# Graph kernel on one core: edge rows made of aligned fours, four gather slots a row, built in the first stage

## The reference

```python
xl, xr, e = x @ Wl.T + bl, x @ Wr.T + br, edge_attr @ We.T
m = xl[src] + xr[dst] + e
score = jnp.where(m > 0, m, 0.2 * m) @ att
es = jnp.exp(score - segment_max(score, dst)[dst])
alpha = es / (segment_sum(es, dst)[dst] + 1e-16)
out = segment_sum(alpha[:, None] * xl[src], dst)
```

## Time and profile before

| | |
|---|---|
| median of 3 runs | 15386.39 us (15376.81 to 15424.71) |
| profiled execution, span | 15438.3 us |
| TensorE, VectorE busy | 7512.3, 6521.2 us (49%, 42%) |
| ScalarE, GpSimd busy | 3580.5, 7851.1 us (23%, 51%) |
| DMA | mean 72 GB/s, 1912984 packets |
| mean granted TensorE clock | 0.605 of full speed |

### The profile page before, as it was taken

How to read it: one execution, slowest core, us unless ns; L and a number is a source line. 1 busy time by engine, 2 the same in 40 slices (tenths; PEclk the granted TensorE clock), 3 DMA queues, 4 the chain that set the end, 5 groups by cost and what they waited for, 6 DMA issues and landing times. The chain is left out here.

```text
span 15438.3 us, 178521 instructions
## 1 busy us (share of the span) xinstructions
PE 7512.3 (49%) x38527; PEld 6783.9 (44%) x38528; DVE 6521.2 (42%) x11789; ACT 3580.5 (23%) x4864; POOL 7851.1 (51%) x8083
## 2 busy tenths in 40 slices
PE   0555555545555555355455554444444434545442
PEld 0544544544455544344444433444444334444442
DVE  3344444444444544333333343444444634434343
ACT  0222222212222222122222212222222122222220
POOL 3455555525555554356556615555455155555551
PEclk9566666656666666555555555555555555665565
DMA  2333333333333333222222233333333243333331
GB/s 69 76 78 80 78 75 76 78 62 80 76 78 78 80 78 62 41 46 47 47 45 49 47 101 82 76 75 78 74 76 76 73 117 83 85 83 85 83 74 22
DMA packets 1912984, 1106.77 MB, mean 72 GB/s; under 512 B 1548686, under 2 KB 1593762, under 8 KB 1911874
## 3 DMA queue, kind: packets, MB, share of 16 engines
q1 hardware_dynamic: 1654786, 718.42, 19.1%
q0 software_dynamic: 257568, 382.66, 12.6%
HBM read 1003.35 MB, written 96.52 MB: 71 GB/s over the span
## 5 line engine op out<-in xcount | busy, mean ns | idle before, releaser
L1006 POOL DMA_INDIRECT ds_gat<-table_d,ds_idx x1568 | 1508.6, 962 | 1562.1 <-issue 803.9
L1006 POOL DMA_INDIRECT as_gat<-table_a,as_idx x1568 | 1529.5, 975 | 1254.5 <-DMA as_idx<-in_srcT 721.1
L1006 POOL DMA_INDIRECT bs_gat<-table_b,bs_idx x1568 | 1538.6, 981 | 1199.0 <-DMA bs_idx<-idx_d 680.0
L1006 POOL DMA_INDIRECT es_gat<-table_e,es_idx x1568 | 1523.7, 972 | 1195.7 <-issue 578.3
L1006 POOL DMA_INDIRECT cs_gat<-table_c,cs_idx x1568 | 1532.7, 978 | 1088.9 <-issue 544.8
L1271 PE MATMUL cs_psA<-cs_ahot,cs_wtd 128*68 128x128 f32 x3136 | 670.8, 400 | 434.0 <-ACT cs_psA L1031 315.3
L1271 PE MATMUL es_psA<-es_ahot,es_wtd 128*68 128x128 f32 x3136 | 619.2, 377 | 406.5 <-ACT es_psA L1031 256.1
L1271 PE MATMUL bs_psA<-bs_ahot,bs_wtd 128*65 128x128 f32 x3136 | 624.2, 361 | 393.8 <-issue 351.3
L1271 PEld LDWEIGHTS cs_psA<-cs_ahot,cs_wtd 128*68 128x68 f32 x3136 | 605.2, 221 | 456.0 <-issue 455.6
L1256 PE MATMUL es_psM<-es_dst,es_hot 128*128 128x64 f32 x3136 | 595.2, 361 | 415.1 <-issue 202.3
L1256 PEld LDWEIGHTS es_psM<-es_dst,es_hot 128*128 128x128 f32 x3136 | 568.7, 275 | 462.2 <-issue 369.8
(11 more groups left out here) (734 smaller groups left out, 16292.6 us busy)
## 6 DMA issues: line engine op xcount, KB each, us to landing
ds_dst<-dst_d SPq DMA_DIRECT2D x1568, 34.0 KB
as_rank<-rel_d SPq DMA_DIRECT2D x196, 256.0 KB
as_dst<-dst_a SPq DMA_DIRECT2D x1568, 32.0 KB
as_ea<-in_eaT SPq DMA_DIRECT2D x196, 256.0 KB
bs_rank<-rel_d SPq DMA_DIRECT2D x196, 256.0 KB
bs_dst<-dst_b SPq DMA_DIRECT2D x1568, 32.0 KB
bs_ea<-in_eaT SPq DMA_DIRECT2D x196, 256.0 KB
cs_rank<-rel_d SPq DMA_DIRECT2D x196, 256.0 KB
```

What stands on the lines that cost most here:

```text
L1006: g_.indirect_dma_start(gat[s][:, j, :], None, table, bass.IndirectOffsetOnAxis(ap=idxS[s][:, j:j + 1].bitcast(U32), axis=0)).then_inc(got ...
```

## The change

Edges are taken four at a time (50000 aligned fours). One row, that is one partition of a tile, is a pair of a four and a destination that occurs in it: it has four gather slots, of which those whose edge has another destination are masked by a penalty (`pen`, -1e37). A four with edges of two destinations makes two rows, so there are at most 50000 + 6249 rows, in T = 440 tiles. A group is 2 tiles, which is again 8 gathers (220 groups), a chunk 8 tiles or four groups (55 chunks). What changes with it:

- `expand` and `collect` work on 2 tiles a group, with one destination window a tile. In a and b the features of the four edges of a row are turned by 4 products (`edges`), copied to SBUF by ScalarE (`eS`), and spread by a second one-hot matrix (`hot`, index 1), since two rows can share a four.
- The maximum over the four slots is taken before the scans (`most`), which so run on a quarter of the partitions. In a, b, c and e the maximum is transposed back (`B`), subtracted from the scores (`lower`) and only then goes through the exponential; in d the scores of all four slots are transposed.
- `weigh` is followed by a sum over the four slots (`wsum`), `flush` handles one tile of 256 columns instead of two of 512.
- `feed` loads the index four groups earlier (`LEAD`); `lag` is 7, in d still 8.
- `prepare` builds the rows on the chip: it counts destinations per four, makes prefix sums, finds by two small gathered searches which fours each tile begins with (`quad`, `lead`), and then, in 55 steps of 8 tiles, loads a window of 128 fours a tile and picks the rows out of it with products (`unpack`, `spans`, `prefix`, `fields`). Indices, types, ranks and masks come from that instead of from the inputs.

The diff, cut to its core:

```diff
+S = 4
+QN = E // S
+GS = 8
+GROUP = GS // S
+CT = 4 * GROUP
+T = -(-(QN + N - 1) // (P * CT)) * CT
...
+                for g in range(VGS):
+                    wait(sp, read, g - 3)
+                    at = load_windows(nc, m["quad"], g * VG, VG, mybir.EngineType.SP, QN - 1)
+                    for j in range(VG):
+                        sp.dma_start(winI[g % 4][:, j, :], t["quads"][bass.ds(at[j], P), :]).then_inc(wind[g % 4], 16)
...
+                def unpack(g):
+                    v.wait_ge(wind[g % 4], (g // 4 + 1) * 16 * VG)
+                    wait(v, vfd, g - 1)
+                    link(v.tensor_copy(winF[g % 2][:, :, 0:3 * S], winI[g % 4][:, :, :]))
...
+                def spans(g):
+                    v.wait_ge(pred, g + 1)
...
+                    v.tensor_tensor(ge[:, :, :], iota, over(lo[:, :], 2, [P, VG, P]), ALU.is_ge)
+                    link(v.tensor_tensor(hot[g % 2][:, :, :], iota, over(hi[:, :], 2, [P, VG, P]), ALU.is_lt))
+                    v.tensor_tensor(hot[g % 2][:, :, :], hot[g % 2][:, :, :], ge[:, :, :], ALU.mult).then_inc(hotted, 1)
...
+                    for j in range(VG):
+                        last = pe.matmul(psV[g % 2][:, j * NF:(j + 1) * NF], hot[g % 2][:, j, :], winF[g % 2][:, j, :], start=True, stop=True)
...
-                    wait(sp, got[s], it * GOT)
-                    sp.dma_start(idxS[s][:, :], idx[:, bass.ds(g * GROUP, GROUP)]).then_inc(idxd[s], 16)
+                    if within(g + LEAD, GROUPS):
+                        feed_idx(*later(it, s, LEAD))
...
+                        quads = load_windows(nc, m["quad"], g * GROUP, GROUP, mybir.EngineType.SP, QN - 1)
+                        for j in range(GROUP):
+                            sp.dma_start(ea[s % 4][:, :, j, :], t["eaT"][:, :, bass.ds(quads[j], P)]).then_inc(eaed[s % 4], 16)
...
-                        for h in range(2):
-                            a.wait_ge(flushed, (k - 2) * 2 + (h + 1))
-                            a.activation(psA[h][0:CW, :], zero[0:CW, :], ACT.Copy).then_inc(zeroed, 1)
+                        a.wait_ge(flushed, k - 1)
+                        a.activation(psA[ks % 2][0:CW, 0:SPAN], zero[0:CW, :], ACT.Copy).then_inc(zeroed, 1)
...
+                def most(c, cs):
+                    v.wait_ge(scored, c * CG + CG)
+                    order = "p s h t -> p h t s" if i == 3 else "p t s h -> p h t s"
+                    v.tensor_reduce(smx[:, :, :], sc[cs][:, :, :, :].rearrange(order), AX_X, ALU.max).then_inc(maxed, 1)
...
+                def lower(xc, xs):
+                    v.wait_ge(backed, xc + 1)
+                    wait(v, alphad, xc)
+                    top = psX[:, BACK:BACK + R].rearrange("p (h t) -> p t h", h=H)
+                    v.tensor_tensor(Dl[:, :, :, :], sc[xs][:, :, :, :], over(top, 2, [P, CT, S, H]), ALU.subtract).then_inc(lowered, 1)
...
+                    v.tensor_reduce(wsum[ks % 2][:, :, :], wtd[:, :, :].rearrange("p (j s) c -> p j c s", s=S), AX_X, ALU.add).then_inc(pooled, 1)
...
+                    for j in range(GROUP):
+                        for x in range(S // 2):
+                            at = (j * (S // 2) + x) * 2 * D
+                            last = pe.matmul(psE[s % 2][:, at:at + 2 * D], ea[s % 4][:, x, j, :], we[:, :], start=True, stop=True)
...
+                            pe.matmul(into, hot[s % 2][:, j, 1, :], eS[s % 2][:, j * S * D:(j + 1) * S * D], start=True, stop=False)
+                            last = pe.matmul(into.rearrange("p (s c) -> p s c", s=S), hot[s % 2][:, j, 0, :],
+                                             over(dsts[s % 4][:, j, :], 1, [P, S, D]), start=False, stop=True)
...
+                    for j in range(GROUP):
+                        last = pe.matmul(at[j], wsum[ks % 2][:, j, :], ahot[ks % 2][:, j, :], start=False, stop=False, skip_group_check=True)
+                    last.then_inc(summed, 1)
```

More of the change, by code:

```diff
@@ L30 @@
 REL = 8
-GROUP = 8
 K = -(-N // P)
@@ new lines, in prepare @@
+        VF = sb("VF", [P, T, NF])
+        kth = sb("kth", [P, T])
+        dl = sb("dl", [P, T, S])
+        val = sb("val", [P, T, S])
+        node = sb("node", [P, T])
+        idxI = sb("idxI", [P, T * S], I32)
+        typI = sb("typI", [P, T * S], I32)
+        nodeT = sb("nodeT", [P, TB, P])
+        new = sb("new", [P, TB, P])
+        cum = sb("cum", [P, TB, P])
+        mask = sb("mask", [P, TB, P], BF16)
+        both = sb("both", [P, TB, 2, P], BF16)
+        tot = sb("tot", [P, 4, TB])
@@ L445, in _ @@
                 pe.wait_ge(made, MADE)
-                pe.wait_ge(sums, 1)
-                pe.matmul(psS[0:ROWS, 0:1], upper[0:ROWS, 0:ROWS], small[0:ROWS, 0:1], start=True, stop=True).then_inc(offs, 1)
-                for b in range(BLK):
-                    pe.wait_ge(back, max(1, b))
-                    pe.transpose(psT[b % 2][:, 0:ROWS], relS[:, b * P:(b + 1) * P], m["ident"][0:ROWS, 0:ROWS]).then_inc(turned, 1)
-                pe.wait_ge(ends, 1)
-                pe.matmul(psS[:, 8:9], pickF[:, :], cumE[:, 0:1], start=True, stop=False)
@@ L454, in _ @@
[L454 to L459 removed]
+                pe.wait_ge(counted, 1)
@@ new lines, in _, with prefix @@
+                pe.matmul(psS[0:EROWS, 0:1], upper[0:EROWS, 0:EROWS], small[0:EROWS, 0:1], start=True, stop=True).then_inc(offs, 1)
+                pe.wait_ge(headed, 1)
+                pe.matmul(psS[:, 8:8 + EROWS], allone[0:EROWS, :], diag[:, :], start=True, stop=True).then_inc(spreadH, 1)
+                def prefix(g):
+                    pe.wait_ge(nqd, g + 1)
+                    wait(pe, hotted, g - 1)
+                    pe.matmul(psP[g % 2][:, 0:VG], upper[:, :], nq[g % 2][:, :], start=True, stop=True).then_inc(pred, 1)
@@ new lines, in fields @@
+                def fields(g):
+                    pe.wait_ge(hotted, g + 1)
+                    wait(pe, taken, g - 1)
+                    for j in range(VG):
+                        last = pe.matmul(psV[g % 2][:, j * NF:(j + 1) * NF], hot[g % 2][:, j, :], winF[g % 2][:, j, :], start=True, stop=True)
+                    last.then_inc(vfd, 1)
+                prefix(0)
+                for g in range(VGS):
+                    if g + 1 < VGS:
+                        prefix(g + 1)
+                    fields(g)
@@ new lines, in _ @@
+                pe.wait_ge(noded, 1)
+                for b, n in blocks():
+                    wait(pe, pulled, b - 1)
+                    pe.transpose(psT[b % 2][0:n, 0:P], node[:, b * P:b * P + n], m["ident"][:, :]).then_inc(turned, 1)
+                    pe.transpose(psT[b % 2][0:n, P:2 * P], VF[:, b * P:b * P + n, 3 * S + 2], m["ident"][:, :]).then_inc(turned, 1)
+                pe.wait_ge(pulled, TB)
+                pe.matmul(psS[:, 128:128 + TB], after[:, :], nodeT[:, :, P - 1], start=True, stop=True).then_inc(shifted, 1)
@@ new lines, in _ @@
+                pe.wait_ge(summed, 1)
+                pe.matmul(psS[:, 144:144 + TB], upper[:, :], tot[:, 0, :], start=True, stop=True)
+                pe.matmul(psS[:, 144 + TB:144 + 2 * TB], allone[:, :], tot[:, 0, :], start=True, stop=True).then_inc(offset, 1)
+                pe.wait_ge(ranked, 2)
+                for b, n in blocks():
+                    wait(pe, back, b - 1)
+                    pe.transpose(psT[b % 2][:, 0:n], new[0:n, b, :], m["ident"][0:n, 0:n]).then_inc(backed, 1)
@@ L462, in masks @@
+                pe.matmul(psS[:, 122:124], allone[:, :], small[:, 2:4], start=True, stop=True).then_inc(placedR, 1)
 def masks(nc, t, d):
@@ L1234, in step @@
                         score(it, s)
+                        if r == CG - 1:
+                            most(it * 3 + c, c)
+                    if i != 3 and r == 2 and live:
+                        lower(xc, xs)
                 rounds(v, step, END)
@@ L1313, in step @@
                         pe.wait_ge(normed, xc + 1)
-                        pe.matmul(psX[:, 256:256 + CT], Al[:, :], m["quart"][:, :], start=True, stop=True).then_inc(backed, 1)
+                        for x in range(S):
+                            last = pe.matmul(psX[:, BACK + x * CT:BACK + (x + 1) * CT], Al[:, x, :], m["quart"][0:R, :], start=True, stop=True)
+                        last.then_inc(backed, 1)
                     if within(k - 1, GROUPS):
```

848 lines of the change are left out of this document (519 added, 329 removed).

## The result

The changed kernel takes 16037.49 us (median of 4 runs, 16021.16 to 16073.24) where the kernel before took 15397.68 us on the same chip: ratio 1.0412, 95% interval 1.0382 to 1.0442. A second measurement on another chip gave 1.0344 (1.0306 to 1.0381). The forecast was 14760 us, the range ended at 15650.

A forecast was written before the change was run, and what follows sets the result against it. Waits bound it, no engine being full: Sync and TensorE crawl while GpSimd issues indirect DMAs without pause. 15438.3 - 969 (streams) + 342 (first stage and masks) = 14811 us, with the profiled execution 52 us above the median: 14760 us, range 13550 to 15650.

The forecast's parts named there:

- What bounds the kernel: Whole kernel: waits, not a full engine; Sync and TensorE slow while GpSimd gathers without pause; VectorE's own work does not slow.
- The crawl: Sync and TensorE during unbroken indirect DMAs of GpSimd: 1.3 to 1.6 us a DMA, up to 5.6 us a product.
- (1) More gathers: Five gather streams: 220 groups instead of 196 at 10.33 us, +1240 us of GpSimd time that nothing hides.
- (2) Sync and the index: Sync's DMAs a group: 11 to 6 or 10 to 4; 721.1 us index wait goes, ring late next, 50 us slack.
- (5) What a group costs: Five layers' groups: 11.7 us in a and b, 10.9 in c and e, 11.5 in d; streams -969 us.
- the two slopes: Layers a, b against c, e: 0.54 us a group, all the products' (0.135 us each) or all Sync's; middle taken.
- (6) The first stage: Building rows in `prepare`: 55 steps at 6 us, +360 us, bounds +215 and +720; with `masks` +342.
- B: Streams: longer gather runs deepen the slowdown, ring stalls replace index stalls; slower, from 11.9 us a group, up to 17380; chance 0.18.
- A, the floor: Streams: gathers hardly stall, 10.5 us a group, 13835 us in all, 13520 at the least; chance 0.32.
- C: Whole kernel: no change, 15395 us, first stage at +720 and groups 0.25 us longer than forecast; chance 0.04.
- D: Groups: VectorE becomes the bound, its 6.7 us plus chain waits passing 10.33 us; no chance of its own given.
- What would show it: New profile: index waits near zero, streams 2400 to 2600 us, `dst` windows 1.4 us, layer a's table near 600 us.

The follow-up runs named there:

- the probe: Kernels without graph work: 500 one-column VectorE memsets beside 96 unbroken indirect gathers of GpSimd, against an idle GpSimd; the 500 take 145.6 us against 15.5 us.
- the two memsets: Two GpSimd memsets of 730 columns put behind each group of eight gathers in the changed kernel; 15179.1 us, 0.9856 of the kernel before.

## Why the prediction was wrong, step by step

- **What bounds the kernel: right about Sync and TensorE, wrong about VectorE.** The crawl beside unbroken gathers is there, but it takes every other engine. The rows on durations could not show it: an operation of VectorE keeps its 690 ns, and the next one is handed out late. The step took durations for pace. In the probe the pace falls from 32 instructions a us (500 in 15.5 us) to 0.7.
- **(1) More gathers: right.** 24 groups more in each layer at GpSimd's 10.33 us, +1240 us; nothing hid them. Against them stands the time above this floor, 196 x 16.9 = 3310 us before and 220 x 10.3 = 2270 us after.
- **(2) Sync and the index: half right.** The index wait went from 721.1 to 90.9 us in layer a and the ring took its place, as named. But "50 us of slack" was no slack: the groups that the ring waits for were frozen with everybody else.
- **(5) What a group costs: the step that failed.** It priced a product at up to 0.135 us and drew the groups from the two slopes: 11.7, 11.7, 10.9, 11.5 and 10.9 us. Measured were 13.08, 13.06, 11.62, 12.52 and 11.70, 12.39 on average where 11.34 was forecast. The streams grew by 191.5 us and did not shrink by 969: 1160 us of error, nearly all of it. The difference between layers a, b and c, e was taken for the price of products and DMAs, and halving the products again, with two operations of VectorE, moved nothing; what a DMA of Sync costs was never measured alone. What the runs show in its place: beside gathers that stop only when they must, a group takes 12.39 us on average, 2.06 above the floor, and with a planned pause of 1.7 us 11.68. The time above the floor did shrink, from 68.6 - 51.65 = 16.9 us over the five layers' groups to 10.3, where the sum needed 5.1.
- **(6) The first stage: right in kind, short by 93 us.** Instead of +342 us the first gather comes 434.9 us later. The 55 steps take 8.7 us each, not 6 (a window of the changed kernel's first stage, then ScalarE's wait for the products, then timeline rows of one step):

```profile
110.00:575.00 465.00, 225.00 (x968) 214.38 (x968) 264.32 (x547) 14.32 (x53) 46.31 (x49) 1.00 0.11 13
```

```profile
ACT pr_VF L430 <- PE pr_psV L647: 432.8, 51, 9.7
```

```profile
450.24 1.23 DVE L505 TENSOR_TENSOR pr_ge<-iota,pr_lo 128x1024 f32<-128x1024 f32 x1
451.38 1.22 DVE L506 TENSOR_TENSOR pr_hot<-iota,pr_hi 128x1024 f32<-128x1024 f32 x1
452.64 1.23 DVE L507 TENSOR_TENSOR pr_hot<-pr_hot,pr_ge 128x1024 f32<-128x1024 f32 x1
...
453.92 3.59 PE L647 MATMUL pr_psV<-pr_winF,pr_hot 128*128 128x15 f32 x16 [3.40 <-DVE pr_hot L507]
...
449.89 3.95 SPq L344 DMA_DIRECT2D pr_winI<-in_quads  x8
```

  VectorE's 4.9 us (448.90 to 453.87) and the eight products' 3.6 us stand behind one another, since the next `unpack` waits for `fields`; I had added up VectorE's part alone. Sync's eight loads, at 3.95 us, were hidden. Beside the first 49 gathers (to 97.9 us) the steps crawled as said: VectorE waited 23.16 and 20.47 us for the first two of them. The later gathers come in sevens with breaks of 26 to 36 us, and the remaining steps all take 8.7 us. The stated upper bound of +720 us does not add up either: with all 55 steps at 13 us the terms give +675.
- **The rivals.** B was the outcome in direction and size, and half in mechanism. "It decides from 11.9 us a group": the layers took 12.39. For 12.4 the prediction has 15940 us; its own terms give 15925, and the missing 112 us are 62 around the streams (93 in the first stage, 31 less elsewhere) and the 52 us by which the profiled execution was to be longer than the others (it was not: 16034.0 and 16037.49). B was given 0.18. Ring stalls did replace the index stalls, and the runs of gathers grew, as B said, from 21 us to (2876.8 - 521.4 - 90.9) / 77 = 29 us. But with the index load put back the runs are (2868.9 - 407.6 - 257.8) / 92 = 24 us and the layer takes the same time, so the longer runs are not what made the groups long. Against B stood layer d, and d did gain most, 14.86 to 12.52 us; it was not enough. A, the floor, did not come: the groups stayed 1.3 to 2.8 us above it, since the crawl takes every engine. C and D did not come: VectorE is busy 43% of the time.
- **What would show it.** Named as signs of B were groups of 12 us and more with TensorE as the releaser. They came with `wtd`, VectorE's, as the releaser. First to last gather at 2400 to 2600 us held for c and e alone. `dst` windows at 1.4 us each nearly all the time held in layer c (median 1.42 us) and not in layer a (median 0.61). The table of layer a was to start near 600 us; its first memset stands at 699.7.

The rule on hidden fetch (the Trainium skill, Runtime: NRT & Kernel Launch, Instruction fetch mechanics) says that a sequencer dispatches more slowly than its memory is refilled. The probes show a pace of instructions that follows GpSimd's gathers in loops of ten and in straight code alike; whether the fetch is what is held up, no run here shows.

What stays open is what in the chip holds the instructions back, why layers a and b take 1.4 us a group more than c and e (Sync's list is the candidate), and why unplanned stalls (75 in layer a, 7.0 us each) do less than planned ones: in that layer 2.75 us above the floor of 10.33 a group, against 1.5 us with the two memsets. A likely reading, argued and not shown, is that the ring's stall comes when the others have long been starved, so that each stall first pays for their restart; the probe's crawl, which lasts 14 us into the silence after 96 gathers, speaks for it.

## What to carry to other kernels

Where GpSimd issues indirect DMAs back to back, look at how many instructions the other engines start per us, not at how long one takes, and try a short idle time on GpSimd behind every few gathers before shortening anybody's list: 1.7 us between groups of eight gave 10.5% here. Measure the pace while the gathers run, not the time until a list is done. Here a wait that went away was given back at the next gate, so a gain must be counted by the time between two groups, never by the wait removed. And a layout that needs 12% more gathers starts 12% behind when the gathers are the floor.

## What was not expected of the hardware

Beside unbroken indirect gathers on GpSimd (1.25 us each) VectorE starts 0.7 small instructions a us where it starts 32 beside an idle GpSimd, alone or in company, in loops or straight code, and after 96 gathers it stays so for another 14 us in which nothing moves. Memsets or plain loads of GpSimd do nothing of the kind: 500 and 492 instructions in 16 us. A break of 0.09 us a gather doubles the pace, 0.25 us brings it to 8.1 a us, and with 0.92 us the 500 take 16.2 us, as good as alone. And idleness paid: the kernel before became 10.5% faster when each of its 980 groups got 1.4 us of GpSimd memsets on top.
